# One decoder layer on one core: feed-forward quantisation behind the mixing operands, keys, query sums and values between the feed-forward steps, and the output product behind the gate projection

## The chip, the cores and the metric

The kernel runs on 1 core of one Trainium2 chip. The metric is the device time of one execution in microseconds (us). A core has TensorE (PE) for matrix products and transposes, VectorE (DVE), ScalarE (ACT) and GpSimd (POOL) for the work between them, and SyncE (SP), which here starts the transfers. Each engine runs its own instructions in the order in which they are written, and waits at semaphores for the others.

## The reference

A batch of 64 sequences of 64 positions with 256 features goes through three blocks, each added to its input:

```python
x = x + attn(layernorm(x))          # state space mixer
x = x + xattn(layernorm(x), ctx)    # attention over a context
x = x + ffn(layernorm(x))           # feed-forward with quantised weights and activations
```

The mixer projects 256 features to a gate `z` (512), to `x` (512), `B` and `C` (128 each) and 8 step widths `dt`; a causal convolution of 4 taps and silu go over `x`, `B`, `C`. Within a sequence of 64 positions the mixing is a causal product: scores `C B^T`, weighted by a decay, times `x * dt`. Then the skip term, the gate, an RMS norm and the output projection. The attention has 16 query heads and 4 key and value heads of 128, an RMS norm over each query and each key, a mask and a softmax. The feed-forward block is

```python
h = silu(bit_linear(x, w_gate)) * bit_linear(x, w_up)
h = rms_norm(h, ln_weight)
return bit_linear(h, w_down)
# bit_linear: activations rounded to 8 bits by the row's largest magnitude, weights to -1, 0, 1
```

with 1024 hidden features.

## The kernel before

The 64 sequences are cut into 32 tiles of 128 rows (two sequences each). The three blocks are a software pipeline, written out by hand: body `i` works on `mn = i + 1` (the mixer's norm and projections), `m = i` (its mixing), `xa = i - 1` (queries, keys, values), `xb = i - 2` (scores, softmax, attention output), `f = i - 3` (the feed-forward steps) and `fb = i - 4` (its last product); where a number is outside 0 to 31 the part is left out. Bodies -1 to 4 and 31 to 35 are written out, 5 to 30 are a loop. Each engine has its own `body`, a list of parts in a fixed order, and this order alone decides what it does next. `after(engine, step, t)` is a wait until step has been done for t tiles. The eight banks of PSUM are M0, M1, M2 (mixer), X0, X1, X2 (attention), F0, F1 (feed-forward).

The parts that matter here:

- PE `m_x_turn` (L1201) transposes the convolved `x`; DVE `m_xdt` (L856) multiplies it by `dt`, and DVE `m_mix` (L847, L850) writes the decayed scores `mbd`. PE `m_mix` (L1210) multiplies the two, and needs both.
- DVE `f_norm` (L778), `f_range` (L948 to L954) and `f_quant` (L959, L961) normalise a tile for the feed-forward block and round it; PE `f_transpose` (L1345) turns it and ACT `f_T_copy` (L654) copies it.
- PE `f_up` 0 and 1 are the two feed-forward steps: each the gate product in F1 (L1357) and the up product in F0 (L1362). ACT `f_tanh` reads F1, DVE `f_gate` (L967, L971) multiplies the two. Step 1 writes the same banks, so its first half waits for L967 of step 0 and its second for L971.
- PE `x_keys` and `x_values` are six products each (L1143 to L1145). DVE `x_kv` (L892) and `x_vb_add` (L896) add the biases.
- PE `x_sums` adds up squares: those of the queries (L1260) and of the mixer's gated output `m_sq` (L1266), both into M2. `x_sums_turn` (L1273) transposes the sums. DVE `m_total` (L872) and `x_q_mean` (L911) read them, then POOL's `m_rms` (L389), `x_rms` (L407), `x_khat` (L398 to L402) and its later parts, up to `m_decay_in` (L383) and `x_norm` (L346) at the head of the next body.
- PE `m_project_bc` (L1160, L1163), `m_project_z` (L1180), `m_output` (L1220), `x_output` in two halves (L1337) and, between them, `x_k_turn` (L1295), which transposes the normalised keys. DVE `x_residual` (L936) waits for the second half. `x_scores` (L1307) opens the next body.

Of the kernel before, what the change touches and what calls it, by code (L numbers as in the profile page):

```python
# [14 lines left out]
P = 128  # L15
# [3 lines left out]
PKW = 32  # L19
NG = P // PKW  # L20
# [41 lines left out]
def decoder_layer(nc, x, ctx_2048, mask, W_in, conv_w, conv_b, dt_bias, A_log, D_param, norm_w, W_out,  # L62
# [7 lines left out]
    with ExitStack() as ctx:  # L70
# [134 lines left out]
        s = {}  # L205
# [561 lines left out]
        def _(dve):  # L767
# [174 lines left out]
            def f_norm(t):  # L942
                normalise(t, x2[:], f_mv, f_xn, s["f_rstd"], s["f_xn"])

            def f_range(t):

                after(dve, s["f_xn"], t + 1)
                v.tensor_reduce(f_sc[:, 0:1], f_xn[:], AX.X, ALU.max, apply_absolute_value=True).then_inc(s["f_am"].sem, 1)  # L948
                after(dve, s["f_am"], t + 1)
                v.tensor_scalar(f_sc[:, 1:2], f_sc[:, 0:1], QUANT_EPS, None, ALU.max).then_inc(s["f_am2"].sem, 1)  # L950
                after(dve, s["f_am2"], t + 1)
                v.reciprocal(f_sc[:, 2:3], f_sc[:, 1:2]).then_inc(s["f_r"].sem, 1)
                after(dve, s["f_r"], t + 1)
                v.tensor_scalar(f_sc[:, 3:4], f_sc[:, 2:3], QMAX, None, ALU.mult).then_inc(s["f_s"].sem, 1)  # L954

            def f_quant(t):

                after(dve, s["f_s"], t + 1)
                v.tensor_scalar(f_xn[:], f_xn[:], f_sc[:, 3:4], ROUND, ALU.mult, ALU.add).then_inc(s["f_q1"].sem, 1)  # L959
                after(dve, s["f_q1"], t + 1)  # L960
                v.tensor_scalar(f_qb[:], f_xn[:], ROUND, None, ALU.subtract).then_inc(s["f_q2"].sem, 1)  # L961
# [62 lines left out]
            def body(mn, m, xa, xb, f, fb, first=None):  # L1024
# [34 lines left out]
                if first == -1:  # L1059
                    w_sum(0)  # L1060
                    dve.wait_ge(s["p_scaled"].sem, 3)
                if f is not None:
                    f_norm(f)
                    f_range(f)
                if m is not None:
                    m_xdt(m)
                    m_mix(m)
                if f is not None:
                    f_quant(f)
                if first == 0:  # L1070
                    w_sum(1)
# [5 lines left out]
                if first == 0:  # L1077
                    w_scale(1)
                    w_round(1)
                if f is not None:  # L1080
                    f_gate(f, 0)
                if first == 1:
                    dve.wait_ge(s["w_attn"].sem, 16 * W_ATTN)
                if xa is not None:
                    x_kv(xa)
                if m is not None:
                    m_total(m)
                if xa is not None:
# [4 lines left out]
                    x_k_sum(xa)  # L1093
                if mn is not None:
                    m_dt(mn)
                if xa is not None:
                    x_vb_add(xa)
                if mn is not None:
                    m_conv_bc(mn)
                if mn is not None:  # L1100
                    m_dt_ratio(mn)
                if f is not None:
                    f_weight(f)
# [34 lines left out]
        def _(pe):  # L1138
# [109 lines left out]
                                  xcT[:, c, :], start=(c == 0), stop=(c == DC - 1))  # L1248
                last.then_inc(x_Q[g].sem, 1)

            def x_sums(xa, m):

                if m is not None:
                    after(pe, s["m_Xdt"], m + 1)
                if xa is not None:
                    after(pe, x_q2[3], xa + 1)
                    for r in range(2):
                        for g in range(NG):
                            j = r * NG + g
                            last = mm(M2[g * PKW:(g + 1) * PKW, 0:2 * P], pick[:, r, :],  # L1260
                                      q2[:, :, 2 * j:2 * j + 2, :].rearrange("p a h s -> p a (h s)"),
                                      start=(r == 0), stop=(r == 1 and m is None))
                if m is not None:
                    after(pe, s["m_sq"], m + 1)
                    for g in range(NG):
                        last = mm(M2[g * PKW:(g + 1) * PKW, 0:P], pick[:, 2, :], m_sq[:, g, :], start=xa is None, stop=True)  # L1266
                last.then_inc(s["x_ss"].sem, 1)

            def x_sums_turn(xa, m):
# [130 lines left out]
            def body(mn, m, xa, xb, f, fb, first=None):  # L1400
# [33 lines left out]
                    x_attend(xb, 1, xa)  # L1434
                if m is not None:
                    m_mix(m, mn)
                if f is not None:
                    f_transpose(f)
                if first == 1:
                    pe.wait_ge(s["p_lo"].sem, 2)  # L1440
                if xa is not None:
                    x_keys(xa)
                if f is not None:
                    f_up(f, 0, xb)
                if first == 0:
                    w_total(1)
                if xa is not None or m is not None:
                    x_sums(xa, m)
                if f is not None:
                    f_up(f, 1, xb)  # L1450
                if xa is not None or m is not None:
                    x_sums_turn(xa, m)
                if mn is not None:
                    m_project_bc(mn)
                if xa is not None:
                    x_values(xa)
                if first == -1:
                    w_total(0)
                if first == 0:
                    pe.wait_ge(s["p_wout"].sem, 1)  # L1460
                if m is not None:
                    m_output(m, xa)
                if mn is not None:
                    m_project_z(mn)
                if xb is not None:
                    x_output(xb, 0)
                if xa is not None:
# [48 lines left out]
```

## Time and profile before

| | |
|---|---|
| median of 3 runs | 1336.02 us (1334.55 to 1340.02) |
| profiled execution | 1337.6 us, its span 1335.2 us |
| busy in the span | PE 93%, weight loads 77%, DVE 79%, ACT 53%, POOL 57% |
| chain that ended last | PE 88%, DVE 3%, POOL 3%, ACT 2% |
| granted TensorE clock, mean | 0.977 |

The span is the profiled stretch from the first instruction to the last. A busy share is an average over the run, with its start and its end. The chain that ended last is followed back from the last instruction, at each step to what released it or to the instruction before it on its engine; its shares say on which engine the time went. The rows further down are of single stretches: in them "idle before" is the time in which the engine stood still ahead of an instruction, with what released it.

### The profile page before, as it was taken

The page shows a single profiled execution, that of the slowest core. Times are in us where ns is not written, and L with a number is a line of the kernel's source. Part 1 is how long each engine was busy: PE and PEld are TensorE (multiplying, and loading weights), DVE is VectorE, ACT ScalarE, POOL GpSimd, SP SyncE. Part 2 cuts the span into 40 slices and gives each one's busy share as a digit, 9 for nine tenths or more (in the row PEclk, how much of TensorE's full clock was granted, in tenths as well). Part 3 has the DMA queues.
Part 4 walks back from the last instruction along what each step waited for, and adds up shares of the span by engine and source line. Part 5 has one row for each costly group of instructions (what it writes and reads, how often), then busy time and mean ns, then how long its engine had stood idle before and what let it go on. Part 6 is the DMA issues. An engine that isn't in the chain of part 4 may idle for free.

```text
span 1335.2 us, 32010 instructions
## 1 busy us (share of the span) xinstructions
PE 1243.1 (93%) x10807; PEld 1028.0 (77%) x10807; DVE 1057.4 (79%) x2581; ACT 711.7 (53%) x1611; POOL 765.6 (57%) x1338
## 2 busy tenths in 40 slices
PE   2689999999999999999999999999999999999965
PEld 2568788887788888878888887887888778888743
DVE  3755888888888888888888888888888888888555
ACT  1345655555565555556655555565555556655432
POOL 2345556766565576656556655655576656556541
PEclk9689999999999999999999999999999999999986
DMA  5500000000000000000000000000000000000000
GB/s 189 172 5 5 10 13 13 13 12 8 4 12 12 12 12 12 12 4 8 12 12 12 12 12 4 8 12 12 12 12 12 8 4 12 12 12 9 5 5 8
DMA packets 25761, 24.37 MB, mean 18 GB/s; under 512 B 7168, under 2 KB 24064, under 8 KB 25472
## 3 DMA queue, kind: packets, MB, share of 16 engines
q1 hardware_dynamic: 23376, 20.79, 5.0%
q10 hardware_dynamic: 2352, 3.15, 0.7%
q8 instruction: 19, 0.31, 0.1%
q14 instruction: 14, 0.11, 0.0%
HBM read 19.74 MB, written 4.19 MB: 18 GB/s over the span
## 4 chain that ended last, share of the span: by engine, by line
PE 88%; DVE 3%; issue 3%; POOL 3%; ACT 2%; DMA 1%; SPq 0%; POOLq 0%; DVEq 0%; ACTq 0%
PE bank L1247 17%; PE bank L1337 16%; PE bank L1329 5%; PE bank L1307 5%; PE bank L1171 4%; PE bank L1180 4%; PE bank L1220 4%; PE bank L1143 2%; PE bank L1357 2%; PE bank L1210 2%; PE bank L1160 2%; PE bank L1362 2%; PE bank L1260 2%; PE bank L1144 2%; PE bank L1188 2%
## 5 line engine op out<-in xcount | busy, mean ns | idle before, releaser
L1247 PE MATMUL bank<-xcT,wq 128*128 128x128 f32 x2048 | 237.9, 277 | 2.3 <-ACT xcT L607 2.3
L1247 PEld LDWEIGHTS bank<-xcT,wq 128*128 128x128 f32 x2048 | 232.7, 193 | 7.1 <-issue 2.9
L1337 PE MATMUL bank<-wo,oT 128*128 128x256 f32 x1024 | 232.0, 380 | 0.0
L1337 PEld LDWEIGHTS bank<-wo,oT 128*128 128x128 f32 x1024 | 190.5, 191 | 23.8 <-issue 0.3
L813 DVE SCALAR_TENSOR_TENSOR xc<-bank,cw,xc 128x124 f32<-128x124 f32 (+2 forms) x576 | 163.5, 339 | 7.9 <-ACT xc L569 1.3
L389 POOL TENSOR_SCALAR ssy<-ssy 128x1 f32<-128x1 f32 x32 | 6.1, 190 | 263.1 <-DVE ssy L872 263.1
L622 ACT ACTIVATE qT<-bank,bqT 128x128 f32<-128x128 f32 x384 | 109.4, 368 | 51.8 <-PE bank L1247 51.5
L407 POOL TENSOR_TENSOR rq<-rq,minus_half 128x16 f32<-128x16 f32 x32 | 93.2, 2913 | 7.8 <-DVE rq L911 7.8
L967 DVE SCALAR_TENSOR_TENSOR h<-h,bank 128x512 f32<-128x512 f32 x64 | 43.9, 686 | 67.2 <-ACT h L661 67.2
L429 POOL TENSOR_TENSOR pr<-pr,mx 128x512 f32<-128x512 f32 x64 | 65.5, 1044 | 52.3 <-DVE mx L930 52.3
L419 POOL TENSOR_TENSOR pr<-pr,mask 128x512 f32<-128x512 f32 x64 | 83.5, 1326 | 16.4 <-DVE pr L918 16.4
L630 ACT ACTIVATE q<-qT 128x512 f32<-128x512 f32 x128 | 79.4, 651 | 1.0
L1329 PE MATMUL bank<-pT,vb 64*128 64x256 f32 x512 | 73.3, 408 | 0.8 <-ACT pT L642 0.8
L1307 PEld LDWEIGHTS bank<-kT,qT 128*64 128x64 f32 x2048 | 63.6, 140 | 11.7 <-issue 11.7
L616 ACT ACTIVATE kT<-bank,qk_w 128x512 f32<-128x512 f32 x32 | 22.0, 688 | 94.9 <-PE bank L1295 94.9
L649 ACT COPY oT<-bank 128x512 f32<-128x512 f32 x128 | 70.8, 627 | 1.8 <-PE bank L1329 1.8
L661 ACT ACTIVATE h<-bank,f_sc 128x512 f32<-128x512 f32 x64 | 43.4, 679 | 50.1 <-PE bank L1357 50.1
L1307 PE MATMUL bank<-kT,qT 128*64 128x64 f32 x2048 | 68.0, 226 | 1.2 <-issue 1.2
L548 ACT COPY x_x<-x 128x256 f32<-128x256 f32 x32 | 13.0, 406 | 101.7 <-DVE x L936 101.7
L1171 PE MATMUL bank<-m_xnT,w_in 128*128 128x128 f32 x512 | 65.8, 282 | 0.0
L424 POOL TENSOR_TENSOR pr<-pr,mx 128x512 f32<-128x512 f32 x64 | 65.6, 1048 | 0.0
L1180 PEld LDWEIGHTS bank<-m_xnT,w_in 128*128 128x128 f32 x512 | 63.8, 196 | 1.6
(216 smaller groups left out, 3049.7 us busy)
## 6 DMA issues: line engine op xcount, KB each, us to landing
x_in<-in_x SPq DMA_DIRECT2D x32, 128.0 KB, 2.0
c_in<-in_ctx SPq DMA_DIRECT2D x32, 128.0 KB, 2.0
out<-x SPq DMA_DIRECT2D x32, 128.0 KB, 1.7
wq<-in_L_xattn_Wq SPq DMA_DIRECT2D x1, 2048.0 KB, 9.9
wo<-in_L_xattn_Wo SPq DMA_DIRECT2D x1, 2048.0 KB, 12.3
w_in<-in_L_attn_W_in SPq DMA_DIRECT2D x1, 1288.0 KB, 8.5
qT<-in_L_ffn_w_gate ACTq DMA_DIRECT2D x1, 1024.0 KB, 9.2
q<-in_L_ffn_w_up ACTq DMA_DIRECT2D x1, 1024.0 KB, 13.1
```

The source lines that it names most:

```text
L407: g.tensor_tensor(rq[:, 1, :], rq[:, 0, :], minus_half[:, :], ALU.pow).then_inc(s["x_rq"].sem, 1)
L419: g.tensor_tensor(pr_half[n], pr_half[n], bcast(mask2[:, :].unsqueeze(1), [P, NPAIR, SEQ]), ALU.add).then_inc(x_s2[n].sem, 1)
L622: last = sc.activation(qT[:, :, 4 * g + n, :], x_Qbank[g][:, n * P:(n + 1) * P].rearrange("p (a n) -> p a n", a=2), ACT.Identity, bias=bqT ...
L630: sc.activation(q2[:, :, 4 * g:4 * g + 4, :], qT[:, :, 4 * g:4 * g + 4, :], ACT.Square).then_inc(x_q2[g].sem, 1)
L649: sc.copy(oT[:, 8 * n:8 * n + 8, a, :], x_Obank[n][a][:, :].rearrange("p (h l) -> p h l", h=8)).then_inc(x_oT[n][a].sem, 1)
L813: last = v.scalar_tensor_tensor(out=o, in0=src, scalar=cw[:, j, TAPS - 1 - back:TAPS - back], in1=o, op0=ALU.mult, op1=ALU.add)
L1171: last = mm(M2[:, j * P:(j + 1) * P], w_in[:, c, DI + j * P:DI + (j + 1) * P], m_xnT[:, c, :], start=(c == 0), stop=(c == DC - 1))
L1180: last = mm(M1[:, j * P:(j + 1) * P], w_in[:, c, j * P:(j + 1) * P], m_xnT[:, c, :], start=(c == 0), stop=(c == DC - 1))
L1247: last = mm(x_Qbank[g][:, (n % 4) * P:(n % 4 + 1) * P], wq[:, c, n * HD:(n + 1) * HD], xcT[:, c, :], start=(c == 0), stop=(c == DC - 1))
L1307: last = mm((X0, X1)[a][u * SEQ:(u + 1) * SEQ, j * SEQ:(j + 1) * SEQ], qT[:, a, 2 * j + u, :], kT[:, j // 2, a * SEQ:(a + 1) * SEQ], start ...
L1329: last = mm(x_Obank[n][a][:, (kv % 2) * 256:(kv % 2 + 1) * 256], vb[rows, kv * HD:(kv + 1) * HD], pT[rows, 2 * kv:2 * kv + 2, :], start=Tr ...
L1337: last = mm(X1[:, 0:D], oT[:, n, :, :], wo[:, n, :], start=(n == 0), stop=(n == NH - 1))
```

## The change

Only the order of parts in the bodies of DVE and PE changes, and PE's `x_sums` is split in two. No operation is added or left out, and ACT, POOL and SP have the same instructions in the same order.

On DVE `m_xdt` and `m_mix` stand ahead of all of the feed-forward quantisation (`f_norm`, `f_range`, `f_quant`), in place of between `f_range` and `f_quant`; `x_kv` stands ahead of `f_gate` 0 and `x_vb_add` right behind it. On PE `x_keys` stands ahead of `f_transpose`, the sums of the queries ahead of step 0, `x_values` and the sums of `m_sq` between the two steps, and `m_project_z` ahead of `m_output`.

```diff
@@ DVE body
+                if m is not None:
+                    m_xdt(m)
+                    m_mix(m)
                 if f is not None:
                     f_norm(f)
                     f_range(f)
-                if m is not None:
-                    m_xdt(m)
-                    m_mix(m)
-                if f is not None:
                     f_quant(f)
...
+                if first == 1:
+                    dve.wait_ge(s["w_attn"].sem, 16 * W_ATTN)
+                if xa is not None:
+                    x_kv(xa)
                 if f is not None:
                     f_gate(f, 0)
-                if first == 1:
-                    dve.wait_ge(s["w_attn"].sem, 16 * W_ATTN)
-                if xa is not None:
-                    x_kv(xa)
+                if xa is not None:
+                    x_vb_add(xa)
                 if m is not None:
                     m_total(m)
...
                 if mn is not None:
                     m_dt(mn)
-                if xa is not None:
-                    x_vb_add(xa)
-                if mn is not None:
                     m_conv_bc(mn)
@@ PE, x_sums split
-            def x_sums(xa, m):
-
+            def x_q_sums(t, m):
                 if m is not None:
                     after(pe, s["m_Xdt"], m + 1)
...
+                after(pe, x_q2[3], t + 1)
...
+                if m is None:
+                    last.then_inc(s["x_ss"].sem, 1)
+
+            def m_y_sums(t, xa):
+                if xa is None:
+                    after(pe, s["m_Xdt"], t + 1)
+                after(pe, s["m_sq"], t + 1)
+                for g in range(NG):
+                    last = mm(M2[g * PKW:(g + 1) * PKW, 0:P], pick[:, 2, :], m_sq[:, g, :], start=xa is None, stop=True)
                 last.then_inc(s["x_ss"].sem, 1)
@@ PE body
+                if first == 1:
+                    pe.wait_ge(s["p_lo"].sem, 2)
+                if xa is not None:
+                    x_keys(xa)
                 if f is not None:
                     f_transpose(f)
-                if first == 1:
-                    pe.wait_ge(s["p_lo"].sem, 2)
-                if xa is not None:
-                    x_keys(xa)
+                if first == 0:
+                    w_total(1)
+                if xa is not None:
+                    x_q_sums(xa, m)
                 if f is not None:
                     f_up(f, 0, xb)
-                if first == 0:
-                    w_total(1)
-                if xa is not None or m is not None:
-                    x_sums(xa, m)
+                if xa is not None:
+                    x_values(xa)
+                if m is not None:
+                    m_y_sums(m, xa)
                 if f is not None:
                     f_up(f, 1, xb)
                 if xa is not None or m is not None:
                     x_sums_turn(xa, m)
                 if mn is not None:
                     m_project_bc(mn)
-                if xa is not None:
-                    x_values(xa)
+                    m_project_z(mn)
...
                 if m is not None:
                     m_output(m, xa)
-                if mn is not None:
-                    m_project_z(mn)
```

PE in the body of the loop, from the mixing product (`mbd,xdt`) to the transpose of the sums (`ident,ssr`), before; `wk` are the keys, `wg` and `wu` the two halves of a step, `q` the squares of the queries:

```order
L1210 MATMUL bank<-mbd,xdt 64x128 x8
...
L1345 MATMUL bank<-identb,f_qb 128x128 x2
...
L1143 MATMUL bank<-wk_hi,c_hi 128x512
...
L1357 MATMUL bank<-wgT,f_qT 128x512 x2
L1362 MATMUL bank<-wuT,f_qT 128x512 x2
...
L1260 MATMUL bank<-q,pick 32x256 x8
L1266 MATMUL bank<-m_sq,pick 32x128 x4
...
L1357 MATMUL bank<-wgT,f_qT 128x512 x2
...
L1362 MATMUL bank<-wuT,f_qT 128x512 x2
L1273 MATMUL bank<-ident,ssr 128x128 x2
```

and of the change, where the lines have moved up by a few (`wv` are the values):

```order
L1207 MATMUL bank<-mbd,xdt 64x128 x8
...
L1140 MATMUL bank<-wk_hi,c_hi 128x512
...
L1345 MATMUL bank<-identb,f_qb 128x128 x2
...
L1255 MATMUL bank<-q,pick 32x256 x8
L1357 MATMUL bank<-wgT,f_qT 128x512 x2
L1362 MATMUL bank<-wuT,f_qT 128x512 x2
...
L1140 MATMUL bank<-wv_hi,c_hi 128x512
...
L1266 MATMUL bank<-m_sq,pick 32x128 x4
...
L1357 MATMUL bank<-wgT,f_qT 128x512 x2
...
L1362 MATMUL bank<-wuT,f_qT 128x512 x2
L1273 MATMUL bank<-ident,ssr 128x128 x2
```

The keys have moved ahead of the transposes of `f_qb`, the query sums ahead of step 0, and six value products stand behind step 0, so the transpose of the sums comes six products later.

DVE in the same body, from the mixer's norm to the gate, before; `xdt` and `mbd` are the operands of the mixing product, `f_xn` and `f_qb` the feed-forward tile:

```order
L778 TENSOR_SCALAR m_xn<-x_in,m_mv 128x256
...
L778 TENSOR_SCALAR f_xn<-x,f_mv 128x256
L948 TENSOR_REDUCE f_sc<-f_xn 128x1
...
L952 RECIPROCAL f_sc<-f_sc 128x1
...
L856 TENSOR_TENSOR xdt<-bank,dts 128x512
L847 TENSOR_TENSOR mbd<-decay,gm 64x8x64
L850 TENSOR_TENSOR mbd<-decay,gm 64x8x64
L959 TENSOR_SCALAR f_xn<-f_xn,f_sc 128x256
...
L961 TENSOR_SCALAR f_qb<-f_xn 128x256
L864 SCALAR_TENSOR_TENSOR yT<-xc,d_ch,bank 128x128 x4
```

and of the change:

```order
L778 TENSOR_SCALAR m_xn<-x_in,m_mv 128x256
...
L856 TENSOR_TENSOR xdt<-bank,dts 128x512
L847 TENSOR_TENSOR mbd<-decay,gm 64x8x64
L850 TENSOR_TENSOR mbd<-decay,gm 64x8x64
...
L778 TENSOR_SCALAR f_xn<-x,f_mv 128x256
L948 TENSOR_REDUCE f_sc<-f_xn 128x1
...
L952 RECIPROCAL f_sc<-f_sc 128x1
...
L959 TENSOR_SCALAR f_xn<-f_xn,f_sc 128x256
...
L961 TENSOR_SCALAR f_qb<-f_xn 128x256
L864 SCALAR_TENSOR_TENSOR yT<-xc,d_ch,bank 128x128 x4
```

The whole feed-forward chain stands behind the three operations that write the operands, and directly ahead of `m_gate` (L864).

DVE behind the gate of the mixer, of the change; `kb` are the keys, `vb` the values, `h` the hidden tile of the feed-forward block:

```order
L868 TENSOR_TENSOR yT<-yT,zs 128x512
L892 TENSOR_TENSOR kb<-bank,bk_r 128x512
L967 SCALAR_TENSOR_TENSOR h<-h,bank 128x512
L971 TENSOR_TENSOR h<-h,bank 128x512
L896 TENSOR_TENSOR vb<-bank,bv_r 128x512
L872 TENSOR_REDUCE ssy<-bank 128x1
L911 TENSOR_SCALAR rq<-bank 128x16
```

Before, `kb` stood behind the two operations on `h`, and `vb` some eight operations further down, ahead of the convolution of `B` and `C`.

## Rows read from the trace of the kernel before

**Rows 1.** Windows: us, busy us of each engine with instructions, PE's granted clock, DMA

```profile
600.00:700.00 100.00, 97.91 (x862) 80.56 (x862) 83.96 (x209) 60.07 (x139) 58.59 (x101) 1.00 0.04 12
```

**Rows 2.** Timeline of PE, steady body: start us, us, instruction, idle before and releaser

```profile
611.36 0.60 PE L1201 MATMUL bank<-ident,xc 128*128 128x128 f32 x4
...
615.15 1.09 PE L1210 MATMUL bank<-mbd,xdt 128*64 128x128 f32 x16 [0.70 <-issue]
...
616.27 0.48 PE L1143 MATMUL bank<-wk_hi,c_hi 128*128 128x512 f32 x1
...
617.76 0.61 PE L1357 MATMUL bank<-wgT,f_qT 128*128 128x512 bf16 x2
...
618.73 1.07 PE L1260 MATMUL bank<-q,pick 128*32 128x256 f32 x16
619.66 0.43 PE L1266 MATMUL bank<-m_sq,pick 128*32 128x128 f32 x8
620.02 0.60 PE L1357 MATMUL bank<-wgT,f_qT 128*128 128x512 bf16 x2
620.59 0.60 PE L1362 MATMUL bank<-wuT,f_qT 128*128 128x512 bf16 x2
621.03 0.38 PE L1273 MATMUL bank<-ident,ssr 128*128 128x128 f32 x2
...
630.96 0.60 PE L1295 MATMUL bank<-ident,kb 128*128 128x128 f32 x4
...
653.78 1.09 PE L1210 MATMUL bank<-mbd,xdt 128*64 128x128 f32 x16 [0.70 <-issue]
```

**Rows 3.** List of waits, whole run: us in total, times, longest us

```profile
PEld bank L1210 <- issue: 30.8, 28, 2.1
...
PE bank L1210 <- issue: 19.2, 28, 0.7
...
PEld bank L1362 <- DVE h L971: 14.9, 32, 0.6
...
PEld bank L1266 <- ACT m_sq L603: 12.4, 31, 1.9
```

**Rows 4.** Timeline of DVE, the same body

```profile
611.21 0.89 DVE L778 TENSOR_SCALAR f_xn<-x,f_mv 128x256 f32<-128x256 f32 x1
...
613.07 0.69 DVE L856 TENSOR_TENSOR xdt<-bank,dts 128x512 f32<-128x512 f32 x1
...
615.47 0.29 DVE L961 TENSOR_SCALAR f_qb<-f_xn 128x256 bf16<-128x256 f32 x1
...
619.85 0.69 DVE L971 TENSOR_TENSOR h<-h,bank 128x512 f32<-128x512 f32 x1
...
627.20 0.87 DVE L798 TENSOR_SCALAR dts<-dts 128x8 f32<-128x8 f32 x1
...
635.05 0.42 DVE L936 TENSOR_TENSOR x<-bank,x_x 128x256 f32<-128x256 f32 x1 [1.51 <-PE bank L1337]
```

**Rows 5.** Timeline of PE, body 2, which has no feed-forward tile

```profile
111.77 0.60 PE L1201 MATMUL bank<-ident,xc 128*128 128x128 f32 x4
...
114.80 1.09 PE L1210 MATMUL bank<-mbd,xdt 128*64 128x128 f32 x16
```

**Rows 6.** Timeline of DVE, body 2

```profile
112.41 0.69 DVE L856 TENSOR_TENSOR xdt<-bank,dts 128x512 f32<-128x512 f32 x1 [0.99 <-PE bank L1201]
```

**Rows 7.** Timeline of ACT, the steady body

```profile
616.50 0.37 ACT L654 COPY f_qT<-bank 128x256 bf16<-128x256 bf16 x1
```

**Rows 8.** Timeline of POOL, the steady body

```profile
621.81 0.19 POOL L389 TENSOR_SCALAR ssy<-ssy 128x1 f32<-128x1 f32 x1 [8.02 <-DVE ssy L872]
...
627.00 1.04 POOL L402 TENSOR_TENSOR kb<-kb,kss 128x512 f32<-128x512 f32 x1
...
637.78 0.23 POOL L346 TENSOR_SCALAR x_mv<-x_mv 128x1 f32<-128x1 f32 x1 [1.64 <-DVE x_mv L774]
```

**Rows 9.** Timeline of PE, body 31

```profile
1245.57 0.66 PE L1295 MATMUL bank<-ident,kb 128*128 128x128 f32 x4 [0.47 <-POOL kb L402]
```

More of the change, by code:

```diff
@@ L1061, in body @@
                     dve.wait_ge(s["p_scaled"].sem, 3)
-                if f is not None:
-                    f_norm(f)
-                    f_range(f)
                 if m is not None:
@@ L1068, in body @@
                 if f is not None:
+                    f_norm(f)
+                    f_range(f)
                     f_quant(f)
@@ L1079, in body @@
                     w_round(1)
-                if f is not None:
-                    f_gate(f, 0)
                 if first == 1:
@@ L1085, in body @@
                     x_kv(xa)
+                if f is not None:
+                    f_gate(f, 0)
+                if xa is not None:
+                    x_vb_add(xa)
                 if m is not None:
@@ L1249, in x_queries @@
                 last.then_inc(x_Q[g].sem, 1)
-            def x_sums(xa, m):
+            def x_q_sums(t, m):
                 if m is not None:
                     after(pe, s["m_Xdt"], m + 1)
-                if xa is not None:
[L1256 to L1262, printed above, removed]
-                if m is not None:
-                    after(pe, s["m_sq"], m + 1)
-                    for g in range(NG):
-                        last = mm(M2[g * PKW:(g + 1) * PKW, 0:P], pick[:, 2, :], m_sq[:, g, :], start=xa is None, stop=True)
+                after(pe, x_q2[3], t + 1)
+                for r in range(2):
+                    for g in range(NG):
+                        j = r * NG + g
+                        last = mm(M2[g * PKW:(g + 1) * PKW, 0:2 * P], pick[:, r, :],
+                                  q2[:, :, 2 * j:2 * j + 2, :].rearrange("p a h s -> p a (h s)"),
+                                  start=(r == 0), stop=(r == 1 and m is None))
+                if m is None:
[6 more added lines that the diff above has]
+                    last = mm(M2[g * PKW:(g + 1) * PKW, 0:P], pick[:, 2, :], m_sq[:, g, :], start=xa is None, stop=True)
                 last.then_inc(s["x_ss"].sem, 1)
@@ L1436, in body @@
                     m_mix(m, mn)
-                if f is not None:
-                    f_transpose(f)
                 if first == 1:
@@ L1443, in body @@
                 if f is not None:
-                    f_up(f, 0, xb)
+                    f_transpose(f)
                 if first == 0:
                     w_total(1)
-                if xa is not None or m is not None:
-                    x_sums(xa, m)
+                if xa is not None:
+                    x_q_sums(xa, m)
+                if f is not None:
+                    f_up(f, 0, xb)
+                if xa is not None:
+                    x_values(xa)
+                if m is not None:
+                    m_y_sums(m, xa)
                 if f is not None:
@@ L1462, in body @@
                     m_output(m, xa)
-                if mn is not None:
-                    m_project_z(mn)
                 if xb is not None:
```

## The prediction

> **What bounds the kernel now.** I read the windows first: over 100 us of the middle PE is busy 97.91 us at a granted clock of 1.00 (2.4 GHz, the upper of its two levels), DVE 84, ACT 60, POOL 59 [rows 1]. So PE sets the pace, the clock has nothing left to give, and what can be won is PE's own idle time. The timeline of PE shows one body (one value of `i`) from one `m_mix` to the next: 615.15 to 653.78, 38.63 us [rows 2]. In it stands one idle time, 0.70 us ahead of L1210, the mixing product `m_mix`. The list of waits has it 28 times with 19.2 us in total [rows 3]; these are the bodies 3 to 30, which have a mixing tile and a feed-forward tile and another tile coming in.
>
> Its releaser is called "issue", so I looked at what `m_mix` needs. On DVE `f_norm` starts at 611.21, the chain of `f_norm` and `f_range` holds DVE until 613.07, and only then come `m_xdt` and `m_mix` (L856, L847, L850), behind which PE starts at 615.15, 2.08 us after 613.07 [rows 2, 4]. PE had finished what `m_xdt` reads much earlier: L1201 starts at 611.36. The control is body 2, which has no feed-forward tile: there `m_xdt` is released by L1201 itself (0.99 idle), and PE goes from L1201 to L1210 in 114.80 - 111.77 = 3.03 us with no idle time [rows 5, 6], against 615.15 - 611.36 = 3.79 us in the steady body [rows 2]. So 1.86 us of feed-forward work ahead of the mixing operands costs PE 0.76 us a body (0.70 idle, the rest in pipelining).
>
> A second, smaller loss: in feed-forward step 1, L1357 takes 620.59 - 620.02 = 0.57 us from start to start, where step 0 and step 1's second half take 0.44 (621.03 - 620.59) [rows 2]. L1362 is waiting for DVE's L971, which ends at 619.85 + 0.69 = 620.54; the list of waits shows it 32 times on the weight load [rows 2 to 4]. That is 0.13 us a body.
>
> **The change on DVE ahead of `m_mix`.** Nothing is added or removed, only order. `m_xdt` now starts when L1201 is done. By body 2 the operands are ready 112.41 + 2.08 = 114.49, while PE starts at 114.80: 0.31 us of slack [rows 5, 6]. Gain 0.76 a body. Let T be the new start of `m_mix`. Ready operands at T - 0.31, then the feed-forward chain: 1.86 us (which includes a stall, below) and `f_quant` 0.68, so the quantised tile is there by T + 2.23 at the latest.
>
> **Keys ahead of the transposes.** `m_mix` and the two transposes take 616.27 - 615.15 = 1.12 us, the keys 617.76 - 616.27 = 1.49 [rows 2]. The transposes fall due about T + 2.52, so `f_quant` is hidden by the keys with 0.3 us to spare. Without that cover its price would be the whole 1.5 us a body. Behind the transposes ACT copies the result, 0.37 us [rows 7]; the query sums (619.66 - 618.73 = 0.93 us [rows 2]) now cover this, and step 0 starts at T + 3.54. The queries' squares and the attention outputs that keys, sums and values wait for come from ACT instructions ahead of 616.50 [rows 7], before T + 2.1: no wait.
>
> **Values and sums between the two steps.** Step 0 takes 618.73 - 617.76 = 0.97, values are six products like the keys, 1.49, then the sum over `m_sq` 0.36, so step 1's first half starts at T + 6.36 and its second at T + 6.80. `f_gate` 0 ended 2.78 us after step 0's start (620.54 - 617.76) [rows 2, 4]. DVE has `m_gate`, then `x_kv` ahead of it now, all before the tanh arrives, so it still ends about T + 6.32: 0.48 before it is needed, and the 0.13 us goes. `m_sq` is ready by 1.90 us after step 0's start (619.66 - 617.76), T + 5.44, before the sum falls due at T + 6.00. The list of waits has `m_sq` as a releaser 31 times [rows 3]; if part of the 0.93 us is that wait, up to 0.08 more is gained. I take 0.
>
> **What is later.** The transpose of the sums, L1273, moves from 5.88 us behind `m_mix` (621.03 - 615.15) to 7.24: 1.36 later. On DVE `m_total` and `x_q_mean` wait for it, on POOL the whole queue stands behind `m_rms`: it idles 8.02 us until 621.81, and then works almost without pause up to L383, before a last wait of 1.64 at 637.78 [rows 8]. Three things hang on that.
> - The key transpose L1295 needs POOL's L402, which ends at 628.04 [rows 8], T + 12.89 before and T + 14.25 after. Its place on PE is 630.96 - 615.15 = 15.81, less 0.13 = 15.68 [rows 2]. Hidden with 1.4 us.
> - `x_norm` on POOL: 1.64 - 1.36 - 0.13 = 0.15 us left. Hidden, barely. Beyond that it would delay `x_mask`, the softmax and with it DVE's way to `m_mix`.
> - DVE: `f_gate` 1 is 1.5 us later against `m_mix`, but `x_vb_add` (of the size of L971, whose 0.69 [rows 4] I take, some 0.6 of it start to start) has moved ahead of it; so DVE reaches `x_residual` some 0.95 later. It waits 1.51 us there for PE [rows 4], which leaves 1.51 - 0.95 - 0.13 = 0.4 us. Hidden.
>
> `m_project_z` ahead of `m_output` gives `m_rms` and `x_q_mean` 1.8 us of cover. `m_output` needs only DVE's two small sums of T + 8, so this edit is worth nothing by itself.
>
> **One port.** DVE's L798, an operation on 8 columns, takes 0.87 us, from 627.20 to 628.07, and ends with POOL's L402 at 628.04 [rows 4, 8]: one engine holds the other up. `f_norm` at 0.89 us [rows 4] looks like such a hold too. In the new order `f_norm` lies where POOL is idle, so the 1.86 us should shrink; I count nothing for it, since it would only add slack. By the row, an operation that meets L402 or L383 costs DVE up to 1.04 us. The operations that now meet L383 read a PSUM bank, like the ones that met POOL's masking before without being stretched.
> The Trainium skill (SBUF — State Buffer, "SBUF: two separate sides") calls this an exclusive lock on a shared port pair, taken by a DVE operation with two SBUF inputs or in a two-port mode; by this rule `m_residual`, with one SBUF tensor, is not held, and the sum stays as it is. The two rows agree with the rule.
>
> **Ends of the run.** Bodies 0 to 2 have no feed-forward tile, but `m_sq`'s wait on PE is up to 1.9 us there [rows 3], and values now lie in it in one of them: about 1 us gained. In body 31 nothing is projected any more between L1273 and L1295, and PE already waits 0.47 us for L402 [rows 9]; with L1273 1.36 later this wait grows by as much. In body 32 much the same, but most of it is made up ahead. I take 1.3 us lost. Bound for both ends together: -2 to +3.
>
> **Sum.** 28 x (0.76 + 0.13) = 24.9, plus 1.0, less 1.3: 24.6 us. The profiled execution took 1337.6 us (span 1335.2 plus 2.4 around it), 1.6 above the median of 1336.02; I assume the same offset, so 1313.0 for a profiled run and 1336.0 - 24.6 = 1311.4 for the median. Changes below 0.5% (6.7 us) are about what a measurement of this kernel cannot tell from none.
>
> **Rivals.**
> - *All of it comes, as above* (0.66): 1306 to 1316. The upper gain is the 0.08 and a better head: 24.6 + 2.2 + 3.
> - *Partly given back* (0.21). The slacks of 0.15 (POOL), 0.3 (`f_quant`) and 0.4 (DVE) are small; one misjudged by 0.5 us costs 0.2 to 0.4 a body, 28 x 0.3 = 8 us: 1314 to 1328, near 1320. For it: three slacks under 0.5. Against: each was worked out at its upper bound.
> - *No change* (0.06). DVE and POOL already run a loop of their own as long as PE's, and the wait moves from `m_mix` to L1201 or L1295. For it: DVE is busy 84% [rows 1]. Against: its idle 1.51 and POOL's 1.64 are waits for PE, so they have room. About 1334.
> - *Slower* (0.07). POOL's queue, started 1.36 late, reaches `x_norm` late by more than its slack. Everything up to the softmax then slips, and `m_mix` with it. From 0.15 late on it eats slack, and beyond a further 0.3 for the operands each 1 us costs 1 us; past 0.89 more it is slower than before. If POOL were 2 us late in all: 28 x (2.0 - 0.45 - 0.89) = 18 us, 1354. Against: the late start is PE's own count and nothing in POOL's queue is new.
>
> **How the numbers follow.** Faster takes the first two cases, 0.87; same takes 0.06; slower 0.07. The likeliest case gives 1311.4, its own range is 1306 to 1316. To hold 8 in 10, the range takes in most of the second case: 1305 to 1325.
>
> **What would show it.** The idle time ahead of L1210 (now L1207) gone in 28 bodies; `m_xdt` released by the transposes of `xc`; the body 37.7 to 37.8 us long; step 1's halves 0.44 apart; POOL's idle time ahead of `x_norm` nearly gone; DVE's wait for the output product about 0.4; a wait of 1.5 to 2 us ahead of L1295 in body 31. The prediction is wrong if a wait appears ahead of the transposes of `f_qb`, of L1357 in step 0 or of the transposes of `x_xn`, or if granted clock falls below 1.00 in the middle.

## The result and the profile after

| | before | changed |
|---|---|---|
| median of 13 runs each | 1336.02 us | 1341.39 us |
| lowest to highest | 1332.73 to 1340.02 | 1339.63 to 1343.44 |
| ratio, 95% interval | | 1.004 (1.0028 to 1.0053) |
| span of the profiled execution | 1335.2 us | 1339.2 us |

The forecast was 1311.4 us in a range of 1305 to 1325. The kernel became 5.4 us slower, which is less than the 0.5% that the prediction called the limit of a measurement; with 13 runs a side its interval leaves out 1. The two profiled executions lie 3.9 us apart (1337.6 and 1341.45), since that of the kernel before was 1.6 above its median and that of the changed kernel was at its median.

The page of the changed kernel, the shares of the chain that ended last:

```profile
PE 57%; POOL 22%; issue 11%; DVE 5%; POOLq 2%; ACT 1%; DMA 1%; SPq 0%; DVEq 0%; ACTq 0%
```

Before, 88% of this chain was PE and 3% POOL. POOL has become part of what sets the end, although its busy time hardly moved.

The windows of the changed kernel over the stretch of [rows 1]:

```profile
600.00:700.00 100.00, 97.48 (x849) 80.37 (x853) 85.37 (x209) 59.42 (x138) 57.98 (x98) 1.00 0.04 10
```

PE is as busy as before and the clock is at its upper level (2.4 GHz) as before. So an idle time has gone and another has come.

The timeline of PE in one steady body of the changed kernel (start us, us, instruction, idle before and releaser), which answers to [rows 2]:

```profile
610.78 0.60 PE L1198 MATMUL bank<-ident,xc 128*128 128x128 f32 x4
...
613.81 1.09 PE L1207 MATMUL bank<-mbd,xdt 128*64 128x128 f32 x16
...
620.28 0.61 PE L1357 MATMUL bank<-wgT,f_qT 128*128 128x512 bf16 x2
620.72 0.59 PE L1362 MATMUL bank<-wuT,f_qT 128*128 128x512 bf16 x2
621.15 0.38 PE L1273 MATMUL bank<-ident,ssr 128*128 128x128 f32 x2
...
639.36 0.41 PE L1229 MATMUL bank<-ident,x_xn 128*128 128x128 f32 x2 [0.81 <-DVE x_xn L778]
...
652.73 1.09 PE L1207 MATMUL bank<-mbd,xdt 128*64 128x128 f32 x16
```

Both forecast gains are there. From L1198 to the mixing product it is 613.81 - 610.78 = 3.03 us with no idle time, where it was 3.79, and step 1's first half takes 0.44 where it took 0.57. But a new idle time of 0.81 us stands ahead of L1229, the transposes of the normalised attention input, and the body is 652.73 - 613.81 = 38.92 us, 0.29 longer than the 38.63 before.

The list of waits of the changed kernel has it in nearly every body:

```profile
PE bank L1229 <- DVE x_xn L778: 23.9, 27, 2.2
```

What makes `x_xn` late shows on DVE, in the timeline of the same body:

```profile
636.33 1.29 DVE L918 TENSOR_TENSOR pr<-bank,rq 128x512 f32<-128x512 f32 x2
637.67 1.44 DVE L778 TENSOR_SCALAR x_xn<-x,x_mv 128x256 f32<-128x256 f32 x1
```

and on POOL, in the timeline of the changed kernel:

```profile
635.62 1.04 POOL L383 TENSOR_TENSOR seg<-causal,dts 128x512 f32<-128x512 f32 x1 [0.30 <-POOL dts L377]
636.74 0.23 POOL L346 TENSOR_SCALAR x_mv<-x_mv 128x1 f32<-128x1 f32 x1
637.06 0.58 POOL L348 TENSOR_TENSOR x_mv<-x_mv,minus_half 128x1 f32<-128x1 f32 x1
637.69 2.55 POOL L419 TENSOR_TENSOR pr<-pr,mask 128x512 f32<-128x512 f32 x2
```

POOL has no idle time left ahead of `x_norm` (L346, L348); it had 1.64 us [rows 8]. L348 ends at 637.64. DVE's L778 needs its result and starts 0.03 later, and in the same moment POOL goes on to the masking, L419, whose scores are ready at 636.33 + 1.29 = 637.62. L778 works on 256 columns and takes 1.44 us. In the kernel before, POOL waited for the scores:

```profile
638.09 0.58 POOL L348 TENSOR_TENSOR x_mv<-x_mv,minus_half 128x1 f32<-128x1 f32 x1
638.97 2.61 POOL L419 TENSOR_TENSOR pr<-pr,mask 128x512 f32<-128x512 f32 x2 [0.30 <-DVE pr L918]
```

and DVE's L778 started before L419 and took 0.40 us (timeline of DVE, kernel before):

```profile
638.81 0.40 DVE L778 TENSOR_SCALAR x_xn<-x,x_mv 128x256 f32<-128x256 f32 x1
```

There L348 ends at 638.67, 0.23 us ahead of the scores (638.90). So POOL stands still once more behind L348, and in that time DVE gets its start.

The same operation grows by 1.04 us when POOL's masking starts with it. The run holds its own control: the first steady bodies of the changed kernel don't have it yet (timeline of DVE, changed kernel):

```profile
210.38 0.41 DVE L778 TENSOR_SCALAR x_xn<-x,x_mv 128x256 f32<-128x256 f32 x1
...
248.51 1.41 DVE L778 TENSOR_SCALAR x_xn<-x,x_mv 128x256 f32<-128x256 f32 x1
```

Timeline of PE, changed kernel, around these two:

```profile
186.68 1.09 PE L1207 MATMUL bank<-mbd,xdt 128*64 128x128 f32 x16
...
224.60 1.09 PE L1207 MATMUL bank<-mbd,xdt 128*64 128x128 f32 x16
...
263.54 1.09 PE L1207 MATMUL bank<-mbd,xdt 128*64 128x128 f32 x16
```

The body without it takes 224.60 - 186.68 = 37.92 us, the next, with it, 38.94. From 248.51 to 1182.55 there are 25 bodies of this kind, so the loss is 25 us. Body 31 is a second control. POOL has no idle time ahead of L346 there either (timeline of POOL, 1220.33), but L348 ends 0.09 ahead of the scores, the masking waits for them and starts at 1221.39, and the normalisation, which starts at 1221.26, takes 0.41. What decides is not the wait for the mean but whether POOL still waits for the scores.

### The profile page after: what moved, and what is told of

Same layout as the page of the kernel before. It is cut to its first block, busy times and chain, and to the rows that moved or that the text cites. A ratio compares the mean times of both kernels' runs of the same rounds, so it can differ in the third digit from the quotient of the medians.

```text
span 1339.2 us, 31978 instructions
## 1 busy us (share of the span) xinstructions
PE 1238.1 (92%) x10775; PEld 1027.4 (77%) x10807; DVE 1078.0 (80%) x2581; ACT 705.3 (53%) x1611; POOL 778.5 (58%) x1338
## 4 chain that ended last, share of the span: by engine, by line
PE 57%; POOL 22%; issue 11%; DVE 5%; POOLq 2%; ACT 1%; DMA 1%; SPq 0%; DVEq 0%; ACTq 0%
PE bank L1244 18%; PE bank L1329 5%; PE bank L1337 3%; DVE x_xn L778 3%; POOL rq L407 3%; PE bank L1140 3%; POOL f_sc L448 2%; PE bank L1255 2%; PE bank L1207 2%; PE bank L1357 2%; PE bank L1141 2%; PE bank L1142 2%; PE bank L1185 2%; POOL kss L400 2%; PE bank L1317 2%
## 5 line engine op out<-in xcount | busy, mean ns | idle before, releaser
L419 POOL TENSOR_TENSOR pr<-pr,mask 128x512 f32<-128x512 f32 x64 | 81.9, 1300 | 8.8 <-DVE pr L918 7.5
L438 POOL TENSOR_SCALAR f_sc<-f_c,f_sc 128x1 f32<-128x1 f32 x32 | 10.2, 319 | 108.1 <-DVE f_sc L952 108.1
L1177 PE MATMUL bank<-m_xnT,w_in 128*128 128x128 f32 x512 | 67.1, 286 | 0.0
L1168 PE MATMUL bank<-m_xnT,w_in 128*128 128x128 f32 x512 | 65.7, 281 | 0.0
```

Of the source, the lines that this page charges most:

```text
L419: g.tensor_tensor(pr_half[n], pr_half[n], bcast(mask2[:, :].unsqueeze(1), [P, NPAIR, SEQ]), ALU.add).then_inc(x_s2[n].sem, 1)
L1177: last = mm(M1[:, j * P:(j + 1) * P], w_in[:, c, j * P:(j + 1) * P], m_xnT[:, c, :], start=(c == 0), stop=(c == DC - 1))
```

## The experiments

Three theories stood against each other. **Port**: POOL's masking and DVE's normalisation can't use SBUF together, and the one holds the other up. **Lateness**: POOL's queue is late, and everything behind it with it. **Order**: the new order on PE or DVE costs the time, and POOL only shows it. Ratios are to runs of the kernel before on the same chip, made beside each experiment (medians of 1336.44 us for the first four kernels, 1336.54 for the next four, 1334.84 for the last). Line numbers move by a few from kernel to kernel.

### The masking behind the normalisation

```diff
+                if xa is not None and xb is not None:
+                    after(pool, s["x_xn"], xa + 1)
                 if xb is not None:
                     x_mask(xb, 0)
```

> The changed kernel with one wait more: POOL starts the masking of the scores (L419) only when DVE has finished its normalisation x_norm (L778, x_xn). Port theory: in the changed kernel L778 takes 1.44 us in place of 0.40 because POOL's L419 starts in the same moment and holds DVE up; with the wait L778 takes 0.40 to 0.45, PE's idle time of 0.81 ahead of the transposes of x_xn goes to 0, the softmax is 0.4 us later, which its slack takes up, and a body falls from 38.92 to 37.8 or 38.1 us: 1312 to 1320 us. Rival (POOL is simply late, and everything behind x_norm with it): the masking is delayed further, L778 stays or PE's wait stays, and the time is 1341 to 1352.

Measured: 1319.11 us, ratio to before 0.9863 (0.9833 to 0.9893). One more wait, and nothing taken away, makes the changed kernel 22 us faster. Timeline of DVE, with the wait in place (L780 is the normalisation here):

```profile
628.20 0.41 DVE L780 TENSOR_SCALAR x_xn<-x,x_mv 128x256 f32<-128x256 f32 x1
```

Timeline of POOL, same kernel:

```profile
627.59 0.58 POOL L348 TENSOR_TENSOR x_mv<-x_mv,minus_half 128x1 f32<-128x1 f32 x1
628.78 2.50 POOL L419 TENSOR_TENSOR pr<-pr,mask 128x512 f32<-128x512 f32 x2 [0.61 <-DVE x_xn L780]
```

POOL is as late as it was and its masking is 0.6 us later still, yet the normalisation is back at 0.41 and PE goes to the transposes of `x_xn` without idle time. A body takes 38.02 us. That rules lateness out and leaves the meeting of the two operations. That what they share is a port of SBUF is the port theory's account of it; these runs show only that the one stands still while the other works.

### The decay operand behind the softmax's subtraction

`m_decay_in` (L383) leaves the head of POOL's body:

```diff
-                if m is not None:
-                    m_decay_in(m)
                 if xa is not None:
                     x_norm(xa)
...
                     x_sub(xb, 1)
+                if m is not None:
+                    m_decay_in(m)
```

> The changed kernel with POOL's m_decay_in (L383, 1.04 us) moved from the head of the body to behind the second x_sub; nothing else is changed. Queue theory: POOL reaches x_norm about 1.0 us earlier, waits for the mean again as in the kernel before, DVE's L778 starts ahead of the masking and takes 0.4, no wait at the transposes of x_xn: a body of 37.7 to 37.9 us, 1309 to 1316 us. Rival (the loss comes from the new order on PE or DVE and not from POOL's lateness): 1338 to 1344, with PE's idle time ahead of the transposes of x_xn unchanged at 0.8.

Measured: 1316.53 us, ratio 0.9849 (0.982 to 0.9879), half a microsecond above the expected range and 24.9 us under the changed kernel's median: the 25 bodies at 1.0. Timeline of POOL in this kernel:

```profile
626.27 0.23 POOL L346 TENSOR_SCALAR x_mv<-x_mv 128x1 f32<-128x1 f32 x1 [1.18 <-DVE x_mv L774]
...
627.46 2.62 POOL L419 TENSOR_TENSOR pr<-pr,mask 128x512 f32<-128x512 f32 x2 [0.30 <-DVE pr L918]
```

Timeline of DVE, same kernel:

```profile
627.30 0.40 DVE L778 TENSOR_SCALAR x_xn<-x,x_mv 128x256 f32<-128x256 f32 x1
```

POOL waits for the mean again (1.18 us) and then for the scores, and the normalisation starts 0.16 ahead of the masking. The orders of PE and DVE are those of the changed kernel, so by themselves they don't cost the time. The body, from the timeline of PE:

```profile
603.58 1.09 PE L1207 MATMUL bank<-mbd,xdt 128*64 128x128 f32 x16
...
606.10 0.28 PE L1345 MATMUL bank<-identb,f_qb 128*128 128x128 bf16 x2
606.32 1.07 PE L1255 MATMUL bank<-q,pick 128*32 128x256 f32 x16
607.32 0.61 PE L1357 MATMUL bank<-wgT,f_qT 128*128 128x512 bf16 x2
...
641.50 1.09 PE L1207 MATMUL bank<-mbd,xdt 128*64 128x128 f32 x16
```

37.92 us, the length of the undisturbed bodies of the changed kernel, and 0.2 more than the 37.74 of the prediction's sum.

### The values back in their old place

```diff
-                if xa is not None:
-                    x_values(xa)
                 if m is not None:
                     m_y_sums(m, xa)
...
                     m_project_z(mn)
+                if xa is not None:
+                    x_values(xa)
```

`x_vb_add` goes back on DVE likewise.

> The changed kernel with one part undone: x_values stands behind m_project_z again and x_vb_add ahead of the convolution of B and C, so that the transpose of the sums is 1.5 us earlier. Queue theory: POOL starts m_rms 1.5 us earlier, has more than 1 us of idle time ahead of x_norm, and the wait at the transposes of x_xn is gone. The gain of 0.76 at the mixing product stays, the 0.13 in step 1 comes back or grows to 0.4 since only the sum over m_sq lies between the steps: a body of 37.9 to 38.3 us, 1313 to 1326 us. Rival (moving the values isn't what makes it slow): 1338 to 1344.

Measured: 1347.81 us, ratio 1.0081 (1.005 to 1.0112). That is outside both expectations. Timeline of POOL and of PE in this kernel:

```profile
645.17 0.23 POOL L346 TENSOR_SCALAR x_mv<-x_mv 128x1 f32<-128x1 f32 x1 [1.46 <-DVE x_mv L774]
```

```profile
625.15 0.60 PE L1358 MATMUL bank<-wgT,f_qT 128*128 128x512 bf16 x2
...
627.05 0.43 PE L1267 MATMUL bank<-m_sq,pick 128*32 128x128 f32 x8 [0.86 <-ACT m_sq L603]
627.41 0.60 PE L1358 MATMUL bank<-wgT,f_qT 128*128 128x512 bf16 x2
627.98 0.60 PE L1363 MATMUL bank<-wuT,f_qT 128*128 128x512 bf16 x2
```

POOL's part came out as expected: 1.46 us of room ahead of `x_norm`, and no long normalisation. From the transpose of the sums to the mean it is 16.55 us again, as in the kernel before, against 15.15 in the changed one: the moved values are what made POOL late. But a different wait opened: without them nothing lies between step 0 and the sum over `m_sq`, PE stands 0.86 us for ACT, and a body takes 39.00 us.

### The keys and the operands alone

The kernel before with only two of the parts: the mixing operands ahead of all of the quantisation on DVE, the keys ahead of the transposes of `f_qb` on PE.

```diff
@@ DVE
+                if m is not None:
+                    m_xdt(m)
+                    m_mix(m)
                 if f is not None:
                     f_norm(f)
                     f_range(f)
-                if m is not None:
-                    m_xdt(m)
-                    m_mix(m)
...
@@ PE
+                if xa is not None:
+                    x_keys(xa)
                 if f is not None:
                     f_transpose(f)
-                if xa is not None:
-                    x_keys(xa)
```

> The kernel before with two parts of the change alone: on DVE the mixing operands ahead of all of the quantisation, on PE the keys ahead of the transposes of f_qb. Expected: the 0.70 ahead of the mixing product goes, but nothing stands any more between the transposes of f_qb and step 0, so that ACT's copy of 0.37 lies open and PE waits 0.5 to 0.65 us ahead of L1357: net 0.1 to 0.25 a body, 1329 to 1333 us. If the query sums ahead of step 0 were not needed as cover: 1314 to 1316.

Measured: 1336.6 us, ratio 0.9999 (0.9985 to 1.0014): no gain, where 3 to 7 us were expected. Timeline of PE:

```profile
614.07 1.09 PE L1209 MATMUL bank<-mbd,xdt 128*64 128x128 f32 x16
...
616.60 0.28 PE L1344 MATMUL bank<-identb,f_qb 128*128 128x128 bf16 x2
617.39 0.59 PE L1356 MATMUL bank<-wgT,f_qT 128*128 128x512 bf16 x2 [0.51 <-issue]
...
652.62 1.09 PE L1209 MATMUL bank<-mbd,xdt 128*64 128x128 f32 x16
```

The 0.70 ahead of the mixing product is gone and 0.51 stands ahead of step 0, where PE has nothing to do until ACT has copied the quantised tile (616.92 to 617.29, timeline of ACT). 38.55 us against 38.63: the stall has moved. The gain needs cover there, work that PE can do in the meantime; in the changed kernel the query sums are that cover.

### POOL made late in the kernel before

Behind L383, one and then two operations of its form and size are added to POOL in the kernel before, each into a tile of its own that nobody reads:

```diff
                 g.tensor_tensor(seg[:], bcast(causal[:, :].unsqueeze(1), [P, NHM, SEQ]),
                                 bcast(dts[:, 9, :].unsqueeze(2), [P, NHM, SEQ]), ALU.mult).then_inc(s["m_R"].sem, 1)
+                g.tensor_tensor(pad0[:], bcast(causal[:, :].unsqueeze(1), [P, NHM, SEQ]),
+                                bcast(dts[:, 9, :].unsqueeze(2), [P, NHM, SEQ]), ALU.mult)
```

> The kernel before with one operation more on POOL, right behind L383 and of its form and size (1.04 us, written to a tile that nobody reads); nothing else is changed. POOL is idle for 1.64 us ahead of x_norm there, so both theories say: no change, 1333 to 1340 us, with the idle time of POOL down to 0.6 and DVE's L778 at 0.40 us.

> The same with two such operations (2.08 us), so that POOL reaches x_norm about 0.45 us late. Port theory: POOL then goes from x_norm to the masking without a pause, takes the port ahead of DVE, L778 goes from 0.40 to 1.3 or 1.45 us, PE waits 0.7 to 1.0 us ahead of the transposes of x_xn: 28 bodies by 0.6 to 1.1 is 17 to 31 us, 1352 to 1368 us, a step far larger than the 0.45. Rival (lateness alone counts): x_xn is 0.45 late, which PE's slack there takes up, and L778 stays at 0.40: 1335 to 1345 us.

Measured: one operation 1338.47 us, ratio 1.0012 (0.9998 to 1.0027), POOL's idle time down from 1.64 to 0.62 and the normalisation at 0.40; two operations 1363.78 us, ratio 1.0206 (1.0179 to 1.0232). Timelines of DVE, PE and POOL with two (here L784 is the normalisation, L1238 its transposes, L425 the masking):

```profile
651.63 1.34 DVE L784 TENSOR_SCALAR x_xn<-x,x_mv 128x256 f32<-128x256 f32 x1 [0.25 <-POOL x_mv L350]
```

```profile
653.22 0.41 PE L1238 MATMUL bank<-ident,x_xn 128*128 128x128 f32 x2 [0.91 <-DVE x_xn L784]
667.07 1.09 PE L1216 MATMUL bank<-mbd,xdt 128*64 128x128 f32 x16 [0.41 <-issue]
```

```profile
651.56 2.55 POOL L425 TENSOR_TENSOR pr<-pr,mask 128x512 f32<-128x512 f32 x2
```

The first microsecond of extra work on POOL costs no more than the noise (the interval takes in 1), the second 25 us. It isn't a slope but a step, and it comes where POOL no longer waits for anything between `x_norm` and the masking: here L350 ends at 651.59 and the scores were there at 651.38. PE loses 0.91 us ahead of the transposes and gets 0.3 of it back at the mixing product, where the wait falls from 0.70 to 0.41; the steady body is 39.44 us long against 38.63. The loss is made here with PE and DVE in their old order.

### The POOL edit alone

The edit of the second experiment, made in the kernel before.

> The kernel before with POOL's m_decay_in behind the second x_sub, the edit of e2_decay_behind_softmax alone. In the kernel before POOL has room ahead of x_norm already, so the queue theory says no change: 1333 to 1339 us. If the edit had a gain of its own (by the softmax or the mixing), it would show here: below 1330.

Measured: 1335.92 us, ratio 0.9997 (0.9983 to 1.0011). The edit has no gain of its own; what it gives in the changed kernel is the room on POOL that the change had used up.

### The output product ahead of the gate projection

The kernel of the second experiment with one part of the change undone:

```diff
                     m_project_bc(mn)
-                    m_project_z(mn)
...
                     m_output(m, xa)
+                if mn is not None:
+                    m_project_z(mn)
```

> The kernel of e2_decay_behind_softmax with one part of the change undone: m_output ahead of m_project_z again. By the timeline m_output's inputs (x_q_mean and m_total) are ready about 7.9 us behind the mixing product and PE gets there at 8.7 or later, so it costs no wait; the passage from m_project_z to m_output took 1.87 us there against 1.78 from m_project_z to the output product before, so up to 0.09 a body or 2.5 us may be gained: 1312 to 1317 us. If the gate projection was needed as cover, 1320 or more.

Measured: 1315.97 us, ratio 0.9851 (0.9829 to 0.9872), and the same 37.92 us a body (603.79 to 641.71 on the timeline of PE). Neither the gain of 2.5 us nor a wait: this part of the change does nothing here.

### The values back, and the square first

On ACT, `m_square` ahead of `f_tanh` 0, in the kernel of the third experiment:

```diff
+                if m is not None:
+                    m_square(m)
                 if f is not None:
                     f_tanh(f, 0)
-                if m is not None:
-                    m_square(m)
```

> The kernel of e3_values_back with one edit more: ACT's m_square ahead of f_tanh 0 in place of behind it. In e3_values_back PE waited 0.86 us at L1267 for m_sq, which ACT made only behind the tanh of step 0, since no values stood in between as cover, and POOL had 1.46 us of room ahead of x_norm. If that is all that made it slow, m_sq is ready 1 us earlier, the wait goes, and a body falls from 39.00 to 37.9 or 38.1: 1316 to 1323 us, with DVE's normalisation at 0.4 us and POOL's room kept. If it stays above 1335, something else in the undone part costs the time.

Measured: 1347.71 us, ratio 1.009 (1.0062 to 1.0118): wrong. Timeline of PE:

```profile
622.08 0.61 PE L1358 MATMUL bank<-wgT,f_qT 128*128 128x512 bf16 x2
...
623.04 0.43 PE L1267 MATMUL bank<-m_sq,pick 128*32 128x128 f32 x8
624.18 0.60 PE L1358 MATMUL bank<-wgT,f_qT 128*128 128x512 bf16 x2 [0.71 <-DVE h L967]
624.91 0.60 PE L1363 MATMUL bank<-wuT,f_qT 128*128 128x512 bf16 x2
```

The wait for `m_sq` is gone and one for the gate has taken its place. From the start of step 0 to that of step 1 it is 624.18 - 622.08 = 2.10 us: the tanh on ACT and the first operation of `f_gate` on DVE take that long, and step 1 writes the bank that they read. Its second half waits for the second operation, L971, in the same way: from the start of step 0 to that of the second half it is 2.83 us in this kernel (624.91 - 622.08), in that of the third experiment (627.98 - 625.15) and in the kernel before (620.59 - 617.76), and L971 ends 0.05 or 0.06 ahead of it each time. So the gate was the limit in the third experiment already, the wait for `m_sq` lay inside it, and taking it away could gain nothing: both bodies are 39.00 us long. Something must lie on PE in the meantime. Before, it was the sums, all of them; with the query sums ahead of step 0, here it is the values. Whether other work of PE would do as well wasn't tried.

## Why the prediction was wrong

**Right: what bounded the kernel, and the two gains.** PE sets the pace, the 1.86 us of quantisation ahead of the operands cost 0.76 a body, and they came back to the hundredth (3.03 us from the transposes of `xc` to the mixing product). Step 1's 0.13 came too. `f_quant`, the copy, `m_sq` and the key transpose were hidden in the steady body, as forecast. Operands were ready with room: DVE waits 1.08 us for the transposes of `xc` (L856, timeline of DVE). DVE's wait ahead of `x_residual` came out at 0.28 where 0.4 was forecast.

**The step that failed** is this one: "`x_norm` on POOL: 1.64 - 1.36 - 0.13 = 0.15 us left. Hidden, barely. Beyond that it would delay `x_mask`, the softmax and with it DVE's way to `m_mix`." Two things were wrong in it.

First, the size. L383 starts 635.62 - 613.81 = 21.81 us behind the mixing product; before, 19.94 (635.09 - 615.15, timeline of the kernel before). It is 1.87 later and not 1.36. The transpose of the sums is 1.46 later (621.15 - 613.81 = 7.34 against 5.88). The rest, 0.4, comes from small POOL operations that stand still beside long ones of DVE. Timeline of POOL, changed kernel:

```profile
628.12 1.25 POOL L448 TENSOR_TENSOR f_sc<-f_sc 128x1 f32<-128x1 f32 x1
...
631.78 0.70 POOL L361 TENSOR_SCALAR dts<-dts 128x8 f32<-128x8 f32 x1
632.56 0.65 POOL L362 TENSOR_TENSOR dts<-dts 128x8 f32<-128x8 f32 x1
```

Alone such an operation takes 0.2 us. L448 ends at 629.37, 0.05 behind DVE's L975 (628.11 + 1.21), and L361 and L362 end as closely behind L991 and L993. The kernel before has such meetings too (L452 with 1.03, L364 with 0.55, L366 with 0.65), so what is new is only that beyond their 0.2 us each these operations cost 2.1 us in place of 1.7.

DVE's mean is there at 636.30 (L774, 636.12 + 0.18), 22.49 behind the mixing product; before it was 22.43, so the mean did not come earlier by the 0.13 of step 1, but 0.06 later. In the kernel before L346 starts 0.20 behind the mean (637.58 and 637.78), which would be 636.50, and it starts at 636.74. In place of 0.15 us of room POOL is 0.24 late, just over the 0.23 by which L348 ended ahead of the scores.

Second, and this is the larger error, the price of running over. I had a lateness of x cost x, less the slack behind it. What it costs is a collision. As long as POOL waits for the scores, DVE's normalisation starts first. As soon as POOL comes from `x_norm` straight to the masking, both start together and the normalisation takes 1.44 us in place of 0.40. The two padded kernels show the step in the kernel before, the added wait removes it in the changed one.

I had the rule at hand. The Trainium skill (SBUF — State Buffer, "SBUF: two separate sides") has one shared port pair for GpSimd and for DVE's operations in a two-port mode or with two SBUF inputs, taken by whichever starts first and kept for its whole length. The runs agree with the hold: the first of L419's two operations ends at about 637.69 + 2.55 / 2 = 638.97, and the normalisation, held up meanwhile, ends at 637.67 + 1.44 = 639.11. On who starts first the recorded starts don't bear the rule out, since DVE's is the earlier by 0.02. I applied the rule to the operations of DVE that would meet L383 and L402, the ones that the change moves against each other. I didn't apply it to the pair that changes only its order of release.

**The rivals.** The one called slower had the place, POOL late at `x_norm` with everything to the softmax behind it, but not the mechanism: PE's wait sits at the transposes of `x_xn` and not at the softmax or the mixing product. By its formula this lateness (0.15 + 0.24 = 0.39, under its 0.45) would have cost nothing. A wait ahead of the transposes of `x_xn` stood among the prediction's signs that it is wrong, and it is the one that came. Its chance of 0.07 was too small for a forecast that named three slacks under 0.5 us; each is a place where a change of kind can lie, and I treated all three as slopes.

**Sizes that were off a little.** An undisturbed body takes 37.92 us and not 37.74. By the rows of the second experiment the transposes of `f_qb` ahead of the query sums take 606.32 - 606.10 = 0.22 where I had 0.09, the query sums 1.00 where I had 0.93, which together is the whole difference. At 28 bodies that is 5 us. The ends, below, are 1.6 us better than taken, so without the collision the sum would have been about 1315; the kernel of the second experiment measured 1316.53, inside the range. In bodies 31 and 32 the wait at the key transpose grew from 0.47 to 0.90 and from 1.93 to 2.33 (timelines of PE, both kernels), with 0.34 more ahead of the output product in body 31: about 1.1 us for the end, where 1.3 was taken. The start gave 2.4 us up to body 2's mixing product (112.37 against 114.80), where 1.0 was taken.

**The balance.** 28 bodies at 38.63 - 37.92 = 0.71 give 19.9 us. 25 of them lose 1.0 by the collision. With -2.4 at the start and +1.1 at the end: -19.9 + 25 - 2.4 + 1.1 = +3.8, and the spans of the profiled executions differ by 4.0. The best kernels of the study are the change with `m_decay_in` moved on POOL: 1316.5 us with the output product behind the gate projection, 1316.0 with it ahead, no difference within the noise, and 1.5% under the kernel before.

## What to carry to other kernels

When an instruction's slack is used up, don't price only the delay. Look at what its engine does next, and at what that next operation shares with the instruction it has just released: here the same POOL instruction released DVE and freed POOL for the operation that holds DVE up, and 0.24 us of lateness cost 1.0 us a body. A wait that looks idle on an engine off the critical path can be what keeps two operations apart, and adding a wait, or moving one independent operation out of the queue, can then be worth more than the reordering itself. And before undoing a part of a reordering, ask what that part covers: here the query sums cover the copy and the values cover the gate, as the fourth, third and last experiments show, and the keys cover the quantisation by the prediction's count alone; no run leaves them in their old place.

## What the hardware showed that was not expected

- Two operations that one completion sets off, on DVE and on POOL, start within 0.02 us of each other by the records (DVE 637.67, POOL 637.69), and DVE, recorded first, is the one held up. In the padded kernel it is POOL first by 0.07 (651.56 and 651.63) with the same outcome. Where the masking starts 0.13 us behind the normalisation (1221.39 and 1221.26, changed kernel) DVE is not held. Which one holds the other can't be read from starts so close; the duration tells it.
- A held normalisation ends 0.13 to 0.16 us behind the POOL operation that it met, whatever that operation is, though alone it takes 0.40 to 0.41. That is so beside L419 (638.97 and 639.11) and beside the padded kernel's L425 (652.84 and 652.97), where the end of the first operation is estimated as half of the record of both, and in the kernel before beside the cast L413, which has one SBUF input, and beside L415, which has two. Timelines of DVE and POOL, kernel before:

```profile
610.81 0.48 DVE L778 TENSOR_SCALAR m_xn<-x_in,m_mv 128x256 f32<-128x256 f32 x1
611.21 0.89 DVE L778 TENSOR_SCALAR f_xn<-x,f_mv 128x256 f32<-128x256 f32 x1
```

```profile
610.28 0.85 POOL L413 CAST c_hi<-xcT 128x256 fp32r<-128x256 f32 x1
611.22 0.73 POOL L415 TENSOR_TENSOR c_lo<-xcT,c_hi 128x256 fp32r<-128x256 f32 x1
```

L413 ends at 611.13 and `m_xn` at 611.29, L415 at 611.95 and `f_xn` at 612.10. `m_xn` grows only from 0.41 to 0.48 because the cast is nearly over when it starts. So a masking with one input would by these rows hold DVE too; that wasn't tried.
